# Row-maximum products moved directly behind the scores, their maxima taken in the same block, in a hand-ordered attention kernel on one core

## What is computed

```python
xs = reshape(gn(x), (B, 1024, 512))              # group norm, 32 groups; "tokens" are chunks of 512 values
q, k, v = (einsum('btc,hcd->bhtd', xs, W) for W in (Wq, Wk, Wv))     # 8 heads of 64
att = softmax(einsum('bhtd,bhsd->bhts', q, k) / 8, axis=-1)          # 1024 x 1024 for each head
out = transpose(einsum('bhts,bhsd->bhtd', att, v)).reshape(B, 1024, 512) @ Wproj + bproj
return x + reshape(out, x.shape)
```

## Time and profile before

| | us |
|---|---|
| three runs, median (lowest to highest) | 4859.68 (4859.32 to 4861.87) |
| the profiled execution: its own time | 4860.69 |
| its span in the trace | 4858.9 |
| TensorE busy, matrix rows | 4610.2 (95%) |
| ScalarE busy | 2864.6 (59%) |
| VectorE busy | 2775.0 (57%) |
| GpSimd busy | 2319.6 (48%) |
| mean granted TensorE clock | 0.997 |

### The profile page before, as it was taken

How to read it: one execution, slowest core, us unless ns; L and a number is a source line. 1 busy time by engine, 2 the same in 40 slices (tenths; PEclk the granted TensorE clock), 3 DMA queues, 4 the chain that set the end, 5 groups by cost and what they waited for, 6 DMA issues and landing times.

```text
span 4858.9 us, 72553 instructions
## 1 busy us (share of the span) xinstructions
PE 4610.2 (95%) x20352; PEld 3496.1 (72%) x20352; DVE 2775.0 (57%) x5284; ACT 2864.6 (59%) x5507; POOL 2319.6 (48%) x1837
## 2 busy tenths in 40 slices
PE   7999999999999999999999999999999999999998
PEld 5777777777777776767767677676776767767675
DVE  5655646556465564655656556465564656646454
ACT  4665746556465564655646566465664746647464
POOL 2444545445454454544545445454544545445455
PEclk9999999999999999999999999999999999999999
DMA  2111111111111111111111111211112111121101
GB/s 70 35 38 56 31 54 36 45 48 32 54 35 50 45 35 53 33 50 43 35 55 36 51 43 30 64 29 54 37 30 63 36 51 34 33 61 36 54 23 52
DMA packets 156933, 212.69 MB, mean 44 GB/s; under 512 B 56544, under 2 KB 57568, under 8 KB 156512
## 3 DMA queue, kind: packets, MB, share of 16 engines
q1 hardware_dynamic: 156512, 207.47, 15.4%
HBM read 105.12 MB, written 34.08 MB: 29 GB/s over the span
## 4 chain that ended last, share of the span: by engine, by line
issue 50%; POOL 42%; PE 6%; POOLq 1%; ACT 1%; DVE 1%; DMA 0%; SPq 0%; ACTq 0%; DVEq 0%
POOL prob_l L999 32%; POOL o L1016 6%; POOL res L1022 3%; PE bank L486 1%; PE bank L529 1%; POOL rstd L991 1%; POOLq L998 1%; PE bank L546 1%; PE bank L658 1%; PE bank L660 1%; PE bank L659 1%; PE bank L540 0%; PE bank L539 0%; POOLq L1015 0%; ACT prob_h L678 0%
## 5 line engine op out<-in xcount | busy, mean ns | idle before, releaser
L999 POOL TENSOR_TENSOR prob_l<-prob,prob_h 128x512 fp32r<-128x512 f32 x1408 | 1797.3, 1288 | 2389.4 <-ACT prob_h L678 2379.4
L678 ACT ACTIVATE prob<-bank 128x512 f32<-128x512 f32 x2048 | 1237.8, 604 | 1633.6 <-PE bank L540 1487.7
L832 DVE TENSOR_REDUCE smax<-bank 128x1 f32<-128x512 f32 x2048 | 1348.7, 684 | 954.8 <-PE bank L546 942.6
L678 ACT ACTIVATE prob_h<-bank 128x512 fp32r<-128x512 f32 x2048 | 1237.2, 604 | 194.3 <-PE bank L660 154.5
L658 PE MATMUL bank<-prob_h,vh 128*128 128x512 f32 x2048 | 832.6, 407 | 109.0 <-ACT acc L749 99.1
L546 PE MATMUL bank<-k_hl,q_hh 128*128 128x512 f32 x2048 | 798.9, 434 | 33.5 <-DVE smax L832 30.6
L539 PE MATMUL bank<-q_hh,k_hl 128*128 128x512 f32 x2048 | 822.6, 402 | 3.0 <-issue 2.1
L540 PE MATMUL bank<-q_lm,k_h 65*128 65x512 f32 x2048 | 812.3, 397 | 0.0
L659 PE MATMUL bank<-prob_h,vl 128*128 128x512 f32 x2048 | 808.0, 395 | 0.0
L660 PE MATMUL bank<-prob_l,vh 128*128 128x512 f32 x2048 | 807.9, 394 | 0.0
L771 DVE TENSOR_TENSOR prob_l<-prob,prob_h 128x512 fp32r<-128x512 f32 x640 | 507.4, 803 | 501.8 <-ACT prob_h L678 501.7
(11 more groups left out here) (58 smaller groups left out, 4360.1 us busy)
## 6 DMA issues: line engine op xcount, KB each, us to landing
xs<-in_x SPq DMA_DIRECT2D x128, 256.0 KB, 2.8
q_hh<-q_hh SPq DMA_DIRECT2D x256, 128.0 KB, 2.2
k_hl<-k_h SPq DMA_DIRECT2D x256, 128.0 KB, 2.4
inv_b<-inv_dram SPq DMA_DIRECT2D x256, 128.0 KB, 2.8
res<-in_x SPq DMA_DIRECT2D x128, 256.0 KB, 2.7
out_x<-res SPq DMA_DIRECT2D x128, 256.0 KB, 2.0
q_lm<-q_lm SPq DMA_DIRECT2D x256, 2.0 KB
den<-acc SPq DMA_DIRECT2D x256, 2.0 KB, 1.7
```

Of the source, the lines that this page charges most:

```text
L678: return nc.scalar.activation(out, ps[ST + bank][:, :], ACT.Exp, scale=SCALE)
L832: nc.vector.tensor_reduce(smax[:, j:j + 1], ps[SM + j % 2][:, :], AX.X, ALU.max).then_inc(rows_used, 1)
L999: nc.gpsimd.tensor_tensor(prob_l[:, r3, :], prob[:, ring2, :], prob_h[:, r3, :].bitcast(F32), ALU.subtract).then_inc(prob_l_pool, 1)
```

## The change

On TensorE the row-score products leave `other_work` and form `row_work`, called in every block directly behind `scores`, ahead of PV and of `other_work`. On VectorE the maxima taken in block i are those of the products of block i, still ahead of `prob_l`. The tables, all waits and all products stay.

```diff
                     entry(kind, a, lo, hi, bk, before, (s.h + (2 if kind == "qn" else 1)) % NH, wait)
+
+            def row_work(s, i):
+
                 per_slot = max_blocks(s.h, s.has_next, s.section == "body" and s.k == 8)
                 for j in range(sum(per_slot[:i]), sum(per_slot[:i + 1])):
...
                         scores((s.k + ahead) % 2, j, ring3(s, i + AHEAD), wait)
+                    row_work(s, i)
                     if i in s.first[0]:
                         other_work(s, i)
...
                     def maxima():
                         nonlocal hj
-                        for _ in range(per_slot[i - 1] if i else 0):
+                        for _ in range(per_slot[i]):
                             take_max(hj, s.heads(BLOCKS, 1, hj + 1))
```

## The result

The changed kernel takes 4994.43 us (median of 4 runs, 4987.48 to 4996.23) against 4859.5 us before (4 runs, 4859.04 to 4861.87): ratio 1.0274, 95% interval 1.0256 to 1.0292. It is 135 us slower, where the forecast was 17 and the range ended at 31 over the kernel before. The profiled execution spans 4994.4 us (4858.9 before), so both traces can be read against these medians.

A forecast was written before the change was run, and what follows sets the result against it. The prediction took TensorE's instruction list plus its holes as the bound. Losses of 33.2 us less gains of 16.3 gave +16.9 on the profiled 4860.7, so 4877.6, or 4877 against the runs' median; range 4853 to 4891 us.

The forecast's parts named there:

- The change of head: Last blocks of a head: ScalarE's chain starts later; losses 14.7 us (heads 1, 2), 7.8 (plain steps), 6.9 (head 7).
- Head 3, block 1: First row product newly waits about 0.5 us for the DMA of k, against 0.25 lost before: loss 3.8 us.
- The gains: Shorter waits at heads 7, 3, 6 and 0, mostly for row maxima: together 16.3 us.
- head 7: Block 8: the second pair of row products no longer waits or starts late; gain 0.7 in 15 batches, 10.5 us.
- between head 3 and head 4: Head 3, block 14: a wait for a maximum goes, but ScalarE's chain limits the gain to 0.16 a batch, 2.4 us.
- the step of head 0: Block 10: its row product slips under TensorE's wait for output work; gain 0.23 in 15 batches, 3.4 us.
- Head 6: Block 8's 0.86 us wait goes, but block 9's second product then needs a late maximum: gain 0.
- Chains within a step: Heads 3, 6, 7, from PV to a later projection: costed at nothing, between -0.23 and +0.46 for each of 45.
- In a block without waits the order costs nothing: Any block without waits: the same products stand back to back, so reordering them costs nothing.
- Rival 3: Dense blocks: PV waits behind GpSimd's remainders, 0.2 us more in each of 128 steps, +26 us, 4902; chance 0.10.
- Rival 4: The change doesn't do what it says: a late maximum removes the 16.3 us of gains, 4893; within Rival 3's 0.10.
- Rival 1: Waits for maxima were the bound and go, ScalarE makes up for its later start: 4816 us; chance 0.07.

The follow-up runs named there:

- Kernel 3: The changed kernel with the row products of blocks 13 and 14 behind PV again and their maxima a block later: 5017.62 us, ratio 1.0321.
- kernel 4: The changed kernel with VectorE making the remainder of block 10 in block 8, behind block 8's maximum, rather than in block 7: 4955.1 us, ratio 1.0194.
- kernel 7: The changed kernel with the plain steps' pair of row products moved from block 9 to block 10: 4962.77 us, ratio 1.0207.
- Kernel 5: The changed kernel with eight filler products ahead of the waiting PV in block 0 of head 0: 4970.23 us, ratio 1.0223.
- kernel 1: The kernel before with only VectorE's maxima moved into the block of their row products, TensorE's order kept: 5025.7 us, ratio 1.0339.
- kernel 8: The kernel before with maxima in their own block in heads 3 and 7, head 7's row products (blocks 0 to 13) ahead of PV, seven fillers: 4835.9 us.
- kernel 9: Control: the kernel before with the same seven fillers in head 0, block 0, and same-block maxima only in head 7, block 14: 4855.89 us.
- kernel 6: The kernel before with same-block maxima in head 3 and, in head 7's blocks 0 to 13, maxima and row products moved, no fillers: 4856.87 us.

## Why the prediction was wrong

**The direction was right, the size was off by a factor of eight.** Point by point:

- *The change of head.* Right. The ScalarE chain kept its 3.3 us and started later by the row products of the block whose PV it starts behind: 0.44 for 0.46, 0.20 for 0.23, 0.51 for 0.46. Kernel 3 took just this away. Losses at the prediction's places were 36 us for 33.2.
- *Head 3, block 1.* The wait is there (0.48 for about 0.5), but the block loses 0.49, where I took off the 0.25 of the old order: 7 us for 3.8.
- *The gains.* Right in head 7 (0.69 for 0.7 in block 8, 0.77 in the step) and between head 3 and head 4 (0.15 for 0.16); the step of head 0 gains 0.29 for 0.23. Head 6 came out at about 0 by luck: block 8 gains 0.72, but block 9 loses 1.1, where I had let the two cancel, and blocks 2 and 12, which I had not looked at, gain. For head 6 I had weighed the Trainium skill, GPSIMD Engine Reference, Key points, by which VectorE contends with GpSimd where it has two SBUF inputs, as the remainder has and a maximum has not. The trace agrees: the remainder at 1149.66 takes 1.67 us beside GpSimd's work, against 0.69 without it at 1048.72, and the maximum right behind it keeps its 0.68.
- **The first step that failed**: "Chains within a step from PV of one block to a projection in a later one (heads 3, 6, 7) have equal numbers at both ends or are held by GpSimd; I cost them at nothing". I looked for chains that end in a projection, in three kinds of step. I did not look in plain and values steps for the chain that this kernel has in every block with row products: each needs the maximum of the product two before it. So their blocks 9 and 10 went in as nothing, under "In a block without waits the order costs nothing"; the new order put a wait there. I read that chain at head 7, block 8, and at head 6, block 9, and stopped. The same check at plain block 9, against VectorE's list, would have shown block 8's maximum behind the remainder of block 10. That wait measured +40 us (kernels 4 and 7 show it), the same in values steps +25 (block 10 shown by the opposite sign in kernel 4, not undone by itself).
- **The second**: a term for TensorE's clock, which is in no part of the prediction. Its waits grew by 0.2 to 0.5 us at places that were already the longest, and ten changes to head 0 for three are followed by a low stretch. Kernel 5 gave back 24 us of the estimated 37.
- *Rival 3, new waits inside the dense blocks*, had the right place of the time and the wrong mechanism. It spoke of PV waiting for GpSimd's remainders; its sum of 3.0 us against 2.3 held, and that wait did not come. PV waits since it stands behind a row product that waits.
- *Rival 4* named just that mechanism, a late maximum "with PV now behind the waiting product", and gave it a price that was wrong. It let such a maximum undo the 16.3 us of gains and no more (4893). The gains stayed, and the new waits in plain and values steps cost 65 us.
- *Rival 1* ("the maxima were the bound") fell twice. Maxima alone made it 3.4% slower (kernel 1). By the Trainium skill, Perfetto Trace Analysis, Optimization Strategy, one starts sooner what the most contended engine's gaps wait for. That was done for VectorE's maxima and the gaps did close (30.6 to 2.5 us); others behind the same queue opened. In heads 3 and 7 alone, with row products moved too in head 7 and the wait at the change to head 0 filled, it gave 20 us against the control (kernels 8 and 9), though head 4 lost 0.70 a step.

**Open.** Head 1, block 3, loses 0.21 to 1.42 us in the changed kernel in the 14 batches where it stands right behind the loop's back edge, and nothing in the first and the last batch, where no back edge stands before it. VectorE's remainder starts late there; I read it in the trace and tried nothing on it. The 12 us are in no term of the prediction. And why a wait of 1.8 us at the change to head 0 is followed by a low stretch in 14 of 15 batches in kernel 6, in 15 of 15 in kernel 3, and in 3 of 15 before, isn't settled: the length of the wait alone doesn't decide.

## What to carry to other kernels

When work is moved ahead on an engine that executes in order, list for every moved instruction what it waits for on the other engine's list, in every kind of step; one table entry that puts it behind a late neighbour costs the wait for all that stands behind it, here PV. Move both ends of a hand-over together, and only in the steps where nothing late stands between: two heads of eight gave 25 us, with a filled wait, and all eight cost 135. On TensorE price a longer wait above its own length as soon as the trace shows low stretches behind waits of that length, and try filler products in it.

## What the hardware showed that I had not expected

- *The clock falls behind single waits in an engine that is 95% busy.* Behind a wait of 2.26 us it did so in 10 of 15 batches of the changed kernel, behind one of 1.76 in 3 of 15 before: the granted clock is 0.50, mostly for 3.4 us, in which a 128x512 product follows the last after 0.43 us for 0.23. Seven or eight useless products in the wait kept it at 1.00, at no cost of their own in the step's length (59.13 and 58.97 us for the step of head 0).
- *A change elsewhere can decide it.* Kernel 6 left the wait itself nearly as it was (1.81 for 1.76 us), and low stretches there went from 3 to 14 of 15 batches; kernel 3, with 1.78 us, had 15.
- *Two engines hold each other up, VectorE by a factor of more than two.* VectorE's remainder takes 0.69 us, and 1.67 beside GpSimd's scaling; a norm takes 0.54 us, and 1.5 beside GpSimd (kernel 3). GpSimd's `rstd`, 128x4, took 1.46 there in the 15 places where VectorE's remainder had started 0.1 us before it, and 1.01 in the 15 where it had started first. The remainder kept its 0.7 beside `rstd` in both.
